# Adapter plus MoE MLP on one core: POOL, ScalarE and VectorE work reordered at one step of the first pair, adapter matmuls moved at one step of the second

## Chip, core and metric

One NeuronCore of a Trainium2 chip runs the whole kernel. The metric is the device time of one execution in microseconds. Five engines are named as the profile names them: PE (TensorE), DVE (VectorE), ACT (ScalarE), POOL (GpSimd) and SP (SyncE, which here only issues DMAs). Each runs its own queue of instructions strictly in order; they meet through semaphores alone.

## What is computed

16 sequences of 512 tokens by 512 features (f32) go through two residual layers. Both pick weights by an id of the sequence.

```
# layer 0, weights by language id
h = relu(x @ W1[lang] + b1[lang])                # 512 -> 128
y = x + h @ W2[lang] + b2[lang]
x = x + layernorm(y) * gamma[lang] + beta[lang]
# layer 1, last 128 output columns by expert id
h = gelu(x @ W1 + b1)                            # 512 -> 2048
x = x + concat(h @ W2 + b2, h @ We[expert] + be[expert])   # 384 + 128
```

## The kernel before

**Precision.** Every f32 operand of a matmul is split in two fp32r parts: `hi`, the value rounded (a cast, mostly on ACT), and `lo`, the value minus `hi` (a subtraction on DVE, some on POOL). A product is then three matmuls, hi x hi, hi x lo, lo x hi (lines 277 to 279). So before PE can use a tile, ACT must have cast it and DVE have subtracted it.

**Order of the work.** The 16 sequences are taken as 8 pairs, and each pair in 8 groups (k = 0 to 7) of the 2048 hidden features. The up projection of a group uses a Strassen-like scheme with seven products, P1 to P7, of six matmuls of 128 x 128 x 512 each: on PE, `pe_step` (line 576) issues P1, P5, then down products of an earlier group (`pe_down`, 24 matmuls for one sequence of the pair), P6, P2, P3, P7, down products again, P4. The seven products want sums of weight blocks (S1 to S4) and of input blocks (T1 to T4).

**First pair.** In it, the weights are prepared for all pairs: SP loads w1(k+1) raw (`load_w1_raw`, L1610 to L1613), POOL makes its four sums (`pool_weight_sums`, L1410 to L1415), ACT casts (`act_w1_hi`, L755), DVE subtracts (`dve_w1_lo`, L1082), SP stores the split weights in DRAM (`keep_w1`, L1620), from where later pairs load them. Two slots (k % 2) take turns, and a raw load waits for the store of the step before last and for P4 of k - 1. w2 goes the same way (`act_w2_hi` L759, `dve_w2_lo` L1087, `keep_w2` L1636); the expert's columns are split by POOL (`pool_expert`, L1397 and L1399).

**The next pair's layer 0.** While PE is at pair i, layer 0 of pair m = i + 1 is computed in between. At k = 0 to 3, four chunks of x transposed per sequence are loaded (`load_xT`, L1533; two slots, so chunk 2 waits until the products on chunk 0 and 1 are done), cast (L669), subtracted (`dve_xT_lo`, L912), and multiplied in pairs (`pe_adapter_ups`, 6 matmuls into the bank `aux`). The table `ADAPTER_UP` gives sequence and chunk for each n. At k = 2 to 5 follow the second adapter products and DVE's addition (`dve_add_adapter`, L925), which takes x + b2 from `x1`. POOL puts it there (`pool_biases`, L1330, L1332: two additions a tile, x + b2 and x + beta). DVE then takes the moments, finishes the layernorm a step later (`dve_finish`, L985), and turns the result in blocks of 32 x 32 (`dve_turns`, L1003). SP stores the turned tiles in DRAM (`keep_turned`, L1657, eight DMAs for a sequence) and later loads them as the transposed blocks B11 to B22 (L1677) of pair m.

**What sets the order around the change.** All orders are written out by hand: one function per engine and step. At the first pair, k = 5:

- POOL (`pool_first_step`, line 1424): both expert parts of k = 4, biases of tiles 2 and 3 of sequence 1, weight sums of w1(6), expert part of k = 5.
- ACT (`act_step`): gelu and cast of C11(5), cast of w1(6), C12, C22, cast of w2(5).
- DVE (`dve_first_step`): the sums C12 and C22, the low part of g C11(5), two finishes (L985), `dve_add_adapter` for tiles 2 and 3 of sequence 1, turns of tiles 2 and 3 of sequence 0, w1_lo(6), w2_lo(5), moments.
- SP: load of w1(6), store and loads of w2, `keep_turned` of sequence 0 (two halves, each waits for DVE's turns), then `keep_w1(5)`. At k = 6: load of w1(7), stores of w1(6) and w2(5), B11, turned tiles of sequence 1, w2(6), and at k = 7 the load of w1(8), by which pair 1 opens.

At pair 1, k = 1, PE runs P1, P5, the adapter up products on chunks 0 and 1 of pair 2, down(1,7) of the first pair, P6, P2, P3, P7. On DVE, at pair 1, k = 0, the order ends with:

```
        dve_g_lo(eng, i, k, C11)
        if m and k == 0:
            dve_xT_lo(eng, m, 0, 0)
            dve_xT_lo(eng, m, 0, 1)
        if k == 0:
            dve_g_lo(eng, before(i), GROUPS - 1, C12)
            dve_g_lo(eng, before(i), GROUPS - 1, C22)
```

and `pe_down` of sequence 1 waits for these two: `eng.wait_ge(dve_glo[b], pr.count(2 * GROUPS, 2 * k + h + 1))`.

Of the kernel before, what the change touches and what calls it, by code (L numbers as in the profile page):

```python
# [26 lines left out]
def build(nc, xT, x, lang, expert, a_w1, a_b1, a_w2, a_b2, a_gamma, a_beta,  # L27
# [153 lines left out]
    pairs = [Pair(n) for n in range(PAIRS)]  # L181
    first, last_pair = pairs[0], pairs[-1]
# [48 lines left out]
    def before(i):  # L231
        return pairs[i.index - 1]

    def seven(i, n):

        return max(0, i.count(GROUPS, n) - 1)
# [334 lines left out]
    def pe_adapter_ups(eng, m, n):  # L571
        b, c = ADAPTER_UP[n]
        pe_adapter_up(eng, m, b, c)
        pe_adapter_up(eng, m, b, c + 1)

    def pe_step(eng, i, m, k):
        if i is first and k == 0:
            pe_first_group(eng, i)
            return
        pe_p1(eng, i, m, k)  # L580
        pe_p5(eng, i, m, k)
        if m and i is not first and k == 1:
            pe_adapter_ups(eng, m, 0)
        if k % 2 == 0:
            if k >= 2:
                pe_down(eng, i, 0, k - 1)
            elif i is not first:
                pe_down(eng, before(i), 0, GROUPS - 1)
        else:
            if k >= 2:  # L590
                pe_down(eng, i, 1, k - 2)
            elif i is not first:
                pe_down(eng, before(i), 1, GROUPS - 1)
        pe_p6(eng, i, m, k)
        pe_p2(eng, i, k)
        if i is first and k == 1:
            pe_adapter_ups(eng, m, 0)
        pe_p3(eng, i, k)
        pe_p7(eng, i, k)
        if m and k in (2, 3):  # L600
            pe_adapter_ups(eng, m, k)
        if m and k in ADAPTER_DOWN:
            b, t = ADAPTER_DOWN[k]
            eng.wait_ge(act_gelu, i.count(4 * GROUPS, 4 * k + C11 + 1))
            pe_adapter_down(eng, m, b, t, up_a)
            eng.wait_ge(dve_c12, seven(i, k + 1))
            pe_adapter_down(eng, m, b, t + 1, up_c)
        if k % 2 == 0:
            if k >= 2:
                pe_down(eng, i, 1, k - 2)  # L610
            elif i is not first:
                pe_down(eng, before(i), 1, GROUPS - 2)
        elif i is last_pair and k == GROUPS - 1:

            pe_down(eng, i, 0, k - 1, (0,))
            pe_p4(eng, i, k)
            pe_down(eng, i, 0, k - 1, (1,))
            return
        else:
            pe_down(eng, i, 0, k - 1)  # L620
        if m and k == 1:
            pe_adapter_ups(eng, m, 1)
        pe_p4(eng, i, k)
# [133 lines left out]
    def act_w2_hi(eng, k):  # L757
        eng.wait_ge(in_w2[k % 2], 16 * (k // 2 + 1))
        eng.copy(w2[:, k % 2, :, HI, PART:D], w2_raw[:, k % 2, :, LO, PART:D]).then_inc(act_w2hi, 1)  # L759
# [35 lines left out]
    def act_step(eng, i, m, k):  # L795
        if i is first and k == 0:
            return
        if i is first and k == 1:
            act_second_step(eng, i, m)
            return  # L800
        if k > 0:
            act_g(eng, i, k - 1, C21)
        elif i is not first:
            act_g(eng, before(i), GROUPS - 1, C21)
        if i is not first and k < GROUPS - 1 and (k > 0 or before(i) is not first):
            load_w1(eng, i, k + 1)
        act_seed_b(eng, i, k)
        if k > 0:
            act_keep_p5(eng, i, k)
        if k == 1:  # L810
            act_keep_u2(eng, i, k)
        if i is first and k % 2 == 1:
            act_w2_hi(eng, k - 1)
        if k == 0 and before(i) is first:
            act_next_blocks(eng, i)
        if k == 0 and i is not first:
            if before(i) is not first:
                for c in range(2):
                    act_t_hi(eng, i, T3, c)
            for c in range(2):  # L820
                act_block_hi(eng, i, B22, c)
            if before(i) is first:
                load_w1(eng, i, k + 1)
                for c in range(2):
                    act_t_hi(eng, i, T3, c)
            act_keep_p5(eng, i, k)
            if m:
                act_aw_hi(eng, m, 0, 0)
            act_keep_u2(eng, i, k)
            for c in range(2):  # L830
                act_t_hi(eng, i, T4, c)
        if m:
            if k in (2, 4):
                act_relu(eng, m, k // 2 - 1)
            if k in (1, 2, 3):
                b, c = ADAPTER_UP[k]
                act_xT_hi(eng, m, b, c)
                act_xT_hi(eng, m, b, c + 1)
            if k > 0 and k in ADAPTER_WEIGHTS:
                act_aw_hi(eng, m, *ADAPTER_WEIGHTS[k])  # L840
            if k == GROUPS - 1:
                for c in range(2):
                    act_block_hi(eng, m, B11, c)
                if i is not first:
                    load_w1(eng, m, 0)
        if k > 1:
            act_keep_u2(eng, i, k)
        if i is first and k == GROUPS - 1:
            act_w1_hi(eng, k + 1)
        act_g(eng, i, k, C11)  # L850
        if i is first and k < GROUPS - 1:
            act_w1_hi(eng, k + 1)
        if m and k == GROUPS - 1:
            for c in range(2):
                act_t_hi(eng, m, T1, c)
        if m and k == 0:
            act_xT_hi(eng, m, 0, 0)
            act_xT_hi(eng, m, 0, 1)
        act_g(eng, i, k, C12)
        if i is first and k == GROUPS - 1:  # L860
            act_w2_hi(eng, k)
        act_g(eng, i, k, C22)
        if i is first and k in (3, 5):
            act_w2_hi(eng, k)
        if m and k == GROUPS - 1 and i is not first:
            act_next_blocks(eng, m)
# [138 lines left out]
    def dve_turns(eng, m, b, t):  # L1005
        dve_turn(eng, m, b, t)
        dve_turn(eng, m, b, t + 1)
# [77 lines left out]
    def dve_w2_lo(eng, k):  # L1085
        eng.wait_ge(act_w2hi, k + 1)
        eng.tensor_tensor(w2[:, k % 2, :, LO, PART:D], w2_raw[:, k % 2, :, LO, PART:D],  # L1087
                          raw(w2[:, k % 2, :, HI, PART:D]), ALU.subtract).then_inc(dve_w2, 1)
# [27 lines left out]
    def dve_first_step(eng, i, m, k):  # L1116
# [51 lines left out]
        if k in ADAPTER_DOWN:  # L1168
            b, t = ADAPTER_DOWN[k]
            dve_add_adapter(eng, m, b, t, up_a)  # L1170
            dve_add_adapter(eng, m, b, t + 1, up_c)
        if k == 5:
            dve_turns(eng, m, 0, 2)
        if k == 2:
            dve_g_lo(eng, i, k - 1, C22)
            dve_g_lo(eng, i, k, C11)
# [22 lines left out]
            dve_turns(eng, m, 0, 0)  # L1199
        if k == 5:  # L1200
            dve_w2_lo(eng, k)
            dve_moments(eng, m, b, t)
        if k == 6:
            dve_g_lo(eng, i, 5, C12)
# [219 lines left out]
    def pool_first_step(eng, i, m, k):  # L1424

        if k == 0:
            for c in range(2):
                pool_t_lo(eng, i, T1, c)
            return
        if k == 1:  # L1430
            pool_expert(eng, i, 0, 1)
            eng.wait_ge(aw_split, m.front(4, 1))
            pool_aw_lo(eng, m, 0, 1)
            pool_expert(eng, i, 1, 0)
            pool_weight_sums(eng, 3)
            return
        if k == 2:
            pool_biases(eng, m, 0, 0)
            pool_biases(eng, m, 0, 1)
            pool_expert(eng, i, 1, 1)  # L1440
            pool_biases(eng, m, 0, 2)
            pool_biases(eng, m, 0, 3)
            return
        pool_roots(eng, m, k)
        if k == 3:
            pool_expert(eng, i, 0, 2)
            pool_weight_sums(eng, 4)
            pool_expert(eng, i, 1, 2)
            pool_expert(eng, i, 0, 3)
            pool_first_bias(eng, 0)  # L1450
            return
        if k == 4:
            pool_biases(eng, m, 1, 0)
        if k % 2 == 1:
            pool_expert(eng, i, 0, k - 1)
            pool_expert(eng, i, 1, k - 1)
        else:
            pool_expert(eng, i, 1, k - 1)
        if k == 5:
            pool_biases(eng, m, 1, 2)  # L1460
            pool_biases(eng, m, 1, 3)
        if k == 4:
            eng.wait_ge(aw_split, m.front(4, 3))
            pool_aw_lo(eng, m, 1, 1)
        pool_weight_sums(eng, k + 1)
        if k == 4:
            pool_biases(eng, m, 1, 1)
            pool_first_bias(eng, 1)
        if k == GROUPS - 1:
            pool_first_w1_lo(eng, 2)  # L1470
            pool_first_w1_lo(eng, 3)
            pool_expert(eng, i, 0, k)
            pool_expert(eng, i, 1, k)
        elif k % 2 == 1:
            pool_expert(eng, i, 0, k)
# [599 lines left out]
```

## Time and profile before

| | |
|---|---|
| runs | 1422.74, 1424.14, 1424.50 us |
| median | 1424.14 us |
| the profiled execution | 1424.01 us |
| its span (first to last instruction) | 1422.2 us |
| PE busy | 1413.5 us (99%) |
| DVE busy | 878.6 us (62%) |
| ACT busy | 588.0 us (41%) |
| POOL busy | 619.2 us (44%) |
| granted TensorE clock, mean | 0.999 |
| HBM traffic | 205 GB/s over the span |

The times of all rows are microseconds from the first instruction of the span; L and a number is a line of the kernel. PE, DVE, ACT and POOL are the engines, SPq the issue of a DMA on SP. `g`, `w`, `xTs` and so on are the names of tiles. A matmul's duration (0.39) is longer than the distance from one start to the next (0.227), since matmuls are pipelined; it is the distance that counts.

### The profile page before, as it was taken

The page shows a single profiled execution, that of the slowest core. Times are in us where ns is not written, and L with a number is a line of the kernel's source. Part 1 is how long each engine was busy: PE and PEld are TensorE (multiplying, and loading weights), DVE is VectorE, ACT ScalarE, POOL GpSimd, SP SyncE. Part 2 cuts the span into 40 slices and gives each one's busy share as a digit, 9 for nine tenths or more (in the row PEclk, how much of TensorE's full clock was granted, in tenths as well). Part 3 has the DMA queues.
Part 4 walks back from the last instruction along what each step waited for, and adds up shares of the span by engine and source line. Part 5 has one row for each costly group of instructions (what it writes and reads, how often), then busy time and mean ns, then how long its engine had stood idle before and what let it go on. Part 6 is the DMA issues. An engine that isn't in the chain of part 4 may idle for free.

```text
span 1422.2 us, 18606 instructions
## 1 busy us (share of the span) xinstructions
PE 1413.5 (99%) x6220; PEld 1163.1 (82%) x6220; DVE 878.6 (62%) x1472; ACT 588.0 (41%) x968; POOL 619.2 (44%) x628
## 2 busy tenths in 40 slices
PE   9999999999999999999999999999999999999999
PEld 6888787888888888888888888888888888888887
DVE  6888785665656756567565675556665576543333
ACT  4843455333543335343343434443345333533231
POOL 5279345451473414734257342563334633351101
PEclk9999999999999999999999999999999999999999
DMA  8755997558765687566774677645876458654332
GB/s 272 254 183 181 236 357 261 173 170 210 255 218 187 173 233 251 196 211 174 232 254 154 211 193 246 239 151 196 228 245 244 150 173 222 201 191 163 134 111 89
DMA packets 273955, 292.37 MB, mean 206 GB/s; under 512 B 129602, under 2 KB 230722, under 8 KB 265796
## 3 DMA queue, kind: packets, MB, share of 16 engines
q1 hardware_dynamic: 264068, 188.15, 44.7%
q10 hardware_dynamic: 9792, 103.03, 19.2%
q8 instruction: 50, 0.82, 0.2%
q14 instruction: 45, 0.37, 0.1%
HBM read 238.70 MB, written 52.43 MB: 205 GB/s over the span
## 4 chain that ended last, share of the span: by engine, by line
PE 94%; SPq 2%; DVE 2%; DMA 2%; issue 0%; POOL 0%; ACT 0%; ACTq 0%; DVEq 0%
PE down L278 15%; PE down L277 15%; PE down L279 15%; PE up_b L278 5%; PE up_b L277 5%; PE up_b L279 5%; PE up_c L277 4%; PE up_c L278 4%; PE up_c L279 4%; PE up_a L278 4%; PE up_a L277 4%; PE up_a L279 4%; SPq L1657 1%; PE aux L277 1%; PE aux L279 1%; PE aux L278 1%
## 5 line engine op out<-in xcount | busy, mean ns | idle before, releaser
L883 DVE TENSOR_TENSOR g<-g_raw,g 128x512 fp32r<-128x512 f32 x256 | 227.5, 916 | 283.8 <-ACT g L664 283.8
L277 PE MATMUL down<-w,g 128*128 128x512 f32 x1024 | 399.0, 390 | 0.1
L278 PE MATMUL down<-w,g 128*128 128x512 f32 x1024 | 398.8, 389 | 0.0
L279 PE MATMUL down<-w,g 128*128 128x512 f32 x1024 | 398.7, 389 | 0.0
L1397 POOL CAST w<-w_raw 128x256 fp32r<-128x256 f32 x125 | 69.8, 559 | 533.0 <-DMA w_raw<-m_we 532.9
L277 PEld LDWEIGHTS down<-w,g 128*128 128x128 f32 x1024 | 192.8, 188 | 41.1 <-DVE w L1087 0.9
L279 PEld LDWEIGHTS down<-w,g 128*128 128x128 f32 x1024 | 192.3, 188 | 40.0
L278 PEld LDWEIGHTS down<-w,g 128*128 128x128 f32 x1024 | 192.5, 188 | 39.8
L638 ACT COPY u<-up_b 128x512 f32<-128x512 f32 x63 | 37.1, 589 | 304.9 <-PE up_b L279 285.2
L664 ACT CAST g<-g_raw 128x512 fp32r<-128x512 f32 x256 | 159.0, 621 | 8.1
L656 ACT ACTIVATE g_raw<-u,m_b_sb 128x512 f32<-128x512 f32 x63 | 45.6, 723 | 236.8 <-PE down L279 221.0
L277 PE MATMUL up_b<-bo,w 128*128 128x512 f32 x336 | 130.7, 389 | 0.0
L278 PE MATMUL up_b<-bo,w 128*128 128x512 f32 x336 | 130.7, 389 | 0.0
L279 PE MATMUL up_b<-bo,w 128*128 128x512 f32 x336 | 130.7, 389 | 0.0
L1399 POOL TENSOR_TENSOR w<-w_raw,w 128x256 fp32r<-128x256 f32 x128 | 113.4, 886 | 28.2 <-ACT w L765 18.2
L906 DVE TENSOR_TENSOR resid<-down,resid 128x512 f32<-128x512 f32 x124 | 81.0, 684 | 39.2 <-PE down L279 39.2
L656 ACT ACTIVATE g_raw<-up_b,m_b_sb 128x512 f32<-128x512 f32 x63 | 43.2, 686 | 137.0 <-PE up_b L279 137.0
L279 PE MATMUL up_c<-bo,w 128*128 128x512 f32 x224 | 87.2, 389 | 0.0
L278 PE MATMUL up_c<-bo,w 128*128 128x512 f32 x224 | 87.1, 389 | 0.0
L277 PE MATMUL up_c<-bo,w 128*128 128x512 f32 x224 | 87.1, 389 | 0.0
L1332 POOL TENSOR_TENSOR xs<-xs,vecs 128x512 f32<-128x512 f32 x56 | 81.6, 1457 | 4.4
L873 DVE TENSOR_TENSOR u<-up_c,u 128x512 f32<-128x512 f32 x63 | 43.5, 690 | 62.2 <-PE up_c L279 55.7
(234 smaller groups left out, 2414.7 us busy)
## 6 DMA issues: line engine op xcount, KB each, us to landing
w<-w_kept ACTq DMA_DIRECT2D x55, 1792.0 KB, 7.5
w<-w_kept SPq DMA_DIRECT2D x56, 768.0 KB, 5.1
w_raw<-m_we SPq DMA_DIRECT2D x128, 128.0 KB, 4.6
out<-resid SPq DMA_DIRECT2D x64, 256.0 KB, 4.7
xTs_raw<-xT SPq DMA_DIRECT2D x56, 256.0 KB, 3.0
xs<-x SPq DMA_DIRECT2D x56, 256.0 KB, 6.3
w_kept<-w SPq DMA_DIRECT2D x8, 1792.0 KB, 8.1
x_turned<-turned SPq DMA_DIRECT2D x112, 128.0 KB, 3.4
```

The costliest lines, as they stand in the source:

```text
L277: eng.matmul(bank, a_hi, b_hi, start=opens, stop=False, skip_group_check=True)
L278: eng.matmul(bank, a_hi, b_lo, start=False, stop=False, skip_group_check=True)
L279: return eng.matmul(bank, a_lo, b_hi, start=False, stop=closes, skip_group_check=True)
L638: eng.copy(u2[:, :], up_b[:, :]).then_inc(act_u2, 1)
L656: eng.activation(values, source, ACT.Gelu, bias=m_b1_sb[:, j:j + 1]).then_inc(act_gelu, 1)
L664: eng.copy(g[:, b, k % 2, h, HI, :], values).then_inc(act_ghi[b], 1)
L873: eng.tensor_tensor(u2[:, :], up_c[:, :], u2[:, :], ALU.add).then_inc(dve_c12, 1)
L883: eng.tensor_tensor(g[:, b, k % 2, h, LO, :], g_raw[:, b, k % 2, h, LO, :], raw(g[:, b, k % 2, h, HI, :]), ALU.subtract).then_inc(dve_glo[ ...
L906: eng.tensor_tensor(resid[:, 1, t, :], down[t][:, :], before_sum[:, 1, t, :], ALU.add).then_inc(dve_out[1], 1)
L1332: eng.tensor_tensor(xs[:, t, :], xs[:, t, :], vec_tile(m, b, BETA), ALU.add).then_inc(pool_xb, 1)
L1397: eng.tensor_copy(hi, values).then_inc(pool_eh[b], 1)
L1399: eng.tensor_tensor(lo, values, raw(hi), ALU.subtract).then_inc(pool_e[b], 1)
```

## The change

Five edits. At the first pair's k = 5: (1) POOL makes the weight sums of w1(6) between the biases of tile 2 and those of tile 3; (2) ACT casts w2(5) right after C11, ahead of w1(6); (3) DVE turns tiles 2 and 3 of sequence 0 after the low parts of w1(6) and w2(5), where it turned them before both. At pair 1's k = 1: (4) PE issues the adapter up products behind P2 instead of behind P5, so after down(1,7) and P6. (5) A constant, `LATE = 2`, names the pairs with the later place; the first pair had it already.

```diff
+    LATE = 2
+
     def pe_step(eng, i, m, k):
...
         pe_p1(eng, i, m, k)
         pe_p5(eng, i, m, k)
-        if m and i is not first and k == 1:
+        if m and i not in pairs[:LATE] and k == 1:
             pe_adapter_ups(eng, m, 0)
...
         pe_p6(eng, i, m, k)
         pe_p2(eng, i, k)
-        if i is first and k == 1:
+        if m and i in pairs[:LATE] and k == 1:
             pe_adapter_ups(eng, m, 0)
         pe_p3(eng, i, k)
         pe_p7(eng, i, k)
...
         act_g(eng, i, k, C11)
+        if i is first and k == 5:
+            act_w2_hi(eng, k)
         if i is first and k < GROUPS - 1:
             act_w1_hi(eng, k + 1)
...
         act_g(eng, i, k, C22)
-        if i is first and k in (3, 5):
+        if i is first and k == 3:
             act_w2_hi(eng, k)
...
             dve_add_adapter(eng, m, b, t, up_a)
             dve_add_adapter(eng, m, b, t + 1, up_c)
-        if k == 5:
-            dve_turns(eng, m, 0, 2)
...
         if k == 5:
             dve_w2_lo(eng, k)
+            dve_turns(eng, m, 0, 2)
             dve_moments(eng, m, b, t)
...
         if k == 5:
             pool_biases(eng, m, 1, 2)
-            pool_biases(eng, m, 1, 3)
         if k == 4:
             eng.wait_ge(aw_split, m.front(4, 3))
             pool_aw_lo(eng, m, 1, 1)
         pool_weight_sums(eng, k + 1)
+        if k == 5:
+            pool_biases(eng, m, 1, 3)
```

## Rows read from the trace of the kernel before

**Rows 1.** The page: busy time of PE, and the chain that ended last, by engine.
```profile
PE 1413.5 (99%) x6220; PEld 1163.1 (82%) x6220; DVE 878.6 (62%) x1472; ACT 588.0 (41%) x968; POOL 619.2 (44%) x628
PE 94%; SPq 2%; DVE 2%; DMA 2%; issue 0%; POOL 0%; ACT 0%; ACTq 0%; DVEq 0%
```

**Rows 2.** Waits of PE: who waited for whom, us in total, times, longest.
```profile
PE aux L277 <- DVE xTs L912: 2.4, 1, 2.4
...
PE up_a L319 <- DVE w L1082: 0.8, 1, 0.8
```

**Rows 3.** PE's timeline, first pair, k = 5 to 6: start, us, instruction, idle before.
```profile
147.40 0.39 PE L279 MATMUL up_b<-bo,w 128*128 128x512 f32 x1
...
149.77 0.74 PE L319 MATMUL up_a<-bo,w 128*128 128x512 f32 x2 [0.81 <-DVE w L1082]
...
151.98 0.50 PE L277 MATMUL down<-w,g 128*128 128x512 f32 x1
```

**Rows 4.** PE's timeline, pair 1, k = 1.
```profile
213.36 0.39 PE L279 MATMUL up_c<-bo,w 128*128 128x512 f32 x1
216.19 0.47 PE L277 MATMUL aux<-xTs,aw 128*128 128x512 f32 x1 [2.44 <-DVE xTs L912]
...
227.42 0.39 PE L277 MATMUL up_c<-bo,w 128*128 128x512 f32 x1
```

**Rows 5.** Stretches: length, then busy us of PE, PEld, DVE, ACT, POOL, then granted clock.
```profile
213.40:221.10 7.70, 5.25 (x17) 3.91 (x16) 3.84 (x6) 5.93 (x10) 0.72 (x2) 0.78 0.98 357
```

**Rows 6.** The chain of waits in order of time, 139 to 216: start, us, what.
```profile
146.24 0.30 SPq L1657
...
148.52 6.43 DMA w_kept<-w
...
176.68 0.56 SPq L1610
...
191.59 1.42 DVE w L1087
...
205.51 9.17 DMA xTs_raw<-xT
```

**Rows 7.** POOL's timeline, first pair, k = 5.
```profile
139.11 1.30 POOL L1330 TENSOR_TENSOR x<-xs,vecs 128x512 f32<-128x512 f32 x1
...
142.07 1.19 POOL L1410 TENSOR_TENSOR w_raw<-a,w_raw 128x256 f32<-128x256 f32 x1
...
145.18 0.74 POOL L1415 TENSOR_TENSOR w_raw<-w_raw 128x256 f32<-128x256 f32 x1
...
146.34 0.74 POOL L1399 TENSOR_TENSOR w<-w_raw,w 128x256 fp32r<-128x256 f32 x1
```

**Rows 8.** ACT's timeline, the cast of w1(6).
```profile
145.96 1.70 ACT L755 CAST w<-w_raw 128x1792 fp32r<-128x1792 f32 x1 [7.67 <-POOL w_raw L1415]
```

**Rows 9.** DVE's timeline, first pair, k = 5.
```profile
144.33 0.68 DVE L925 TENSOR_TENSOR x<-up_c,x 128x512 f32<-128x512 f32 x1
144.93 1.29 DVE L1003 STREAM_TRANSPOSE turned<-x 128x512 f32<-128x512 f32 x2
147.69 2.03 DVE L1082 TENSOR_TENSOR w<-w_raw,w 128x1792 fp32r<-128x1792 f32 x1 [1.47 <-ACT w L755]
150.97 0.96 DVE L1087 TENSOR_TENSOR w<-w_raw,w 128x768 fp32r<-128x768 f32 x1 [1.26 <-ACT w L759]
```

**Rows 10.** PE's timeline, the first down product at pair 1, k = 0.
```profile
193.06 0.50 PE L277 MATMUL down<-w,g 128*128 128x512 f32 x1
```

**Rows 11.** Line L1082 over the run: duration in ns, least, median, most.
```profile
L1082 DVE TENSOR_TENSOR w<-w_raw,w x7: 1984/2015/3107, 38.9 to 166.9; 128x1792 fp32r<-128x1792 f32 x7
```

**Rows 12.** DVE's timeline, pair 1, k = 0, behind the xT splits.
```profile
216.64 1.28 DVE L883 TENSOR_TENSOR g<-g_raw,g 128x512 fp32r<-128x512 f32 x2
```

**Rows 13.** First pair, k = 1: SP's loads of xT, ACT's casts of them.
```profile
47.17 0.81 SPq L1533 DMA_DIRECT2D xTs_raw<-xT  x2
...
51.92 1.14 ACT L669 CAST xTs<-xTs_raw 128x512 fp32r<-128x512 f32 x2
```

## The prediction

> **What bounds the kernel now.** I read the page first. TensorE (PE) is busy for 1413.5 of 1422.2 us and holds 94% of the chain that ended last [rows 1]. So the end moves only where PE gains or loses time. The next view is the list of what PE waited for. It is short: the longest wait is 2.4 us for a low part of xT (DVE L912), and 0.8 us stands for a low part of w1 (L1082) [rows 2]. The change touches both, and everything after them is PE at its own pace, so a microsecond won or lost here reaches the end whole. Something over 0.2% (2.85 us) is what a measurement of this kernel can tell from no change.
>
> PE's pace is 0.227 us a matmul. In the first pair, up to down(1,5) of k=6, PE starts a matmul at 147.40; thirteen paces on would be 150.35, but the thirteenth starts at 151.98 [rows 3]. So **stall A** costs 1.63 us: P1 waited for the low part of w1(6), the down products for that of w2(5). At pair 1, k=1, the last matmul of P5 starts at 213.36 and the 43rd after it (first of P3) at 227.42 where 43 paces give 223.11 [rows 4]. So **stall B** costs 4.31 us. Only 2.6 of these are the wait; about 1.7 are matmuls at the half clock: the granted clock of 213.4 to 221.1 is 0.78, half of it at 1.2 GHz after the idle time, where it is full elsewhere [rows 5].
>
> The third view is the chain of waits in order of time. It leaves PE at k=5 of the first pair and comes back only at stall B. The links are: the two turns of batch 0 end at 146.2; SP issues their stores (L1657), then the store of w1(5), which lands after 6.43 us; only then may SP load w1(7); SP issues without rest until w1(8) at 176.68; then POOL's sums, ACT's and DVE's splits, among them w2_lo(7) at 191.59; then at 205.51 the load of xT(0,0), 9.17 us [rows 6]. I take from this that the turns of batch 0, tiles 2 and 3, start a path of 60 us in which nearly nothing waits for anything outside it.
>
> **The change, part by part.**
>
> *The weight sum before the last bias.* POOL's stretch is bias(1,2) from 139.11, bias(1,3) to 142.1, four sums from 142.07 to 145.92, then the expert's parts [rows 7]. Swapped, the sums take 3.85 us and end at about 143.0, and bias(1,3) ends where the sums ended, at 145.9; POOL's total doesn't change. ACT's cast of w1(6), 1.7 us [rows 8], is then done at 144.7 in place of 147.7. But DVE's add_adapter(1,3) waits for bias(1,3) (pool_xb, both of its additions), and it stands ahead of w1_lo in DVE's queue. It ran at 144.33 [rows 9]; now it runs at 145.95 to 146.6. So the gain of 3 us on ACT reaches DVE as one of about 1.1: w1_lo(6) takes 2.03 us and ends at 148.6 instead of 149.7.
>
> *w2_hi(5) earlier on ACT, w2_lo(5) behind w1_lo(6).* ACT is idle there, so the 0.8 us cost nothing; w2_lo(5) takes 0.96 [rows 9] and ends at 149.5. P1 of k=6 wants its low part four paces after 147.62, at 148.5, and the down products want w2_lo at 150.35. So stall A shrinks from 1.63 to 0.1: **gain 1.5 us**, at that place.
>
> *The turns behind the low parts.* They took 1.29 us from 144.93 [rows 9]. Now they come last: 145.95 + 0.68 (add) + 2.03 + 0.96 + 1.29, less 3 x 0.08 by which such instructions overlap, is 150.65, against 146.22. SP gets them **D = 4.4 us later**. What is queued behind that wait on SP is what the chain shows: the four stores, the store of w1(5), and behind its landing the loads of w1(7), w2(6) and w1(8). Each takes its time again, so w2_lo(7) ends at 193.01 + 4.4 = 197.4. The down products of the first pair's k=7 began at 193.06, directly after it, with no slack [rows 10]. PE thus stands 4.4 late there whatever stall A gave back: the 1.5 us are swallowed. The bounds of D: 2.9 if add(1,3) waited for nothing (then only 2.0 and 0.96 stand before the turns); 5.5 if w1_lo took the 3.11 us it once took beside POOL [rows 11]. I take 4.4 because the median of the seven w1_lo is 2.02.
>
> Beside it stands a rule. Here w1_lo would start at 146.6, when POOL's split of the expert weights (146.34, 0.74 us [rows 7]) has begun. The Trainium skill, "SBUF — State Buffer", section "SBUF: two separate sides", says that a DVE instruction with two SBUF inputs and a GpSimd one that reads SBUF take one port pair as an exclusive lock: whoever starts first keeps it for the whole instruction. By it w1_lo would start at 147.1 and D be 4.9; the 3.11 us row agrees that DVE can be held up, and the range holds it.
>
> *Adapter up products behind P2 (pair 1, k=1).* PE's order becomes down(1,7), P6, P2, up products, P3. The 24 + 6 + 6 matmuls give xT 8.2 us more. But down(1,7) needs the low part of g C12(7), and in DVE's queue that split stands directly **behind** the two xT splits: it starts at 216.64, the first of two [rows 12], and is done at 217.3. So in the old frame PE, free at 213.6, now waits until 217.35 instead of 216.19. The wait isn't removed, it is 1.16 us longer. From the restart to P3 the work is 42 matmuls either way, 9.52 us; with the same 1.7 us of half clock P3 begins at 217.35 + 9.52 + 1.71 = 228.58 against 227.42: **cost 1.16**. DVE's own path to 216.64 goes through w2_lo(7) and the load of xT, so it carries D too.
>
> Behind that, the load of xT(0,2) waits for the moved products (they free its slot), and the next up products come only P3 + P7 + down(0,0) = 36 matmuls = 8.16 us later, not 16.3. In the first pair, where the order is already so, SP issued this load at 47.17 and ACT split it at 51.92 [rows 13]; 4.75 + 1.14 + 1.28 is under 8.16, so I cost it at nothing. With the 9.17 us of rows 6 in its place it would be 11.4, a stall of some 3 us.
>
> **Sum.** Stall A -1.5, but +1.5 again before 193 (the low part of w2(7) decides); D +4.4; the new wait +1.2: +5.6 us. The profiled execution took 1424.01 us, 0.1 under the median of the runs (1424.14) and 1.8 longer than its span. 1424.0 + 5.6 = **1429.6 us**.
>
> **The rivals.**
> 1. *Forecast, 0.62*: 1429.6. Its own range is D's 2.9 to 5.5, and 2 us more or 1.7 less for the clock: 1426.4 to 1432.7.
> 2. *SP's path has slack for D* (the stores of turned tiles and of w1(5) go faster when nothing else moves, or w1(7) isn't what the later steps wait for). Then only the longer wait at down(1,7) is left: 1424.0 + 1.2 = 1425.2. For it: the 6.43 us of the store of w1(5) were shared with the turned tiles, so one link can shrink; against it: the chain has no wait outside SP and its transfers from 146 to 177. 0.13.
> 3. *xT lands sooner*: with 4.75 us in place of 9.17 the splits come 4.4 earlier, the g split is ready when PE comes 4.4 late, and stall B is gone: 1424.0 + 4.4 - 4.3 = 1424.1, no change. Against it: the same queue of loads stands before it, moved as a whole. 0.07.
> 4. **Faster.** The mechanism is the one of parts 1 and 4 together: w1(8) and w2(7) aren't late, and xT's splits are no longer what PE meets, as DVE's order would allow if they had been done before 213.6. Then stall B goes whole: 1424.0 - 4.3 = 1419.7. It decides if w2_lo(7) is less than 1.4 us late (so that less than that is given back of 4.3) and the g split is done by then. Against it: rows 10 and 12. 0.10.
> 5. *The second xT load is late as well* (9.17 us landing): 1429.6 + 2.8 = 1432.4. 0.08.
>
> Faster is case 4, same (1421.3 to 1427.0) cases 2 and 3, slower cases 1 and 5. The range reaches down to case 3, and up a little past case 5: 1423.8 to 1433.5; it leaves out case 4 and the tails of 1 and 5.
>
> **What would show it.** In the changed profile: L1082 of k=6 at about 146.6; the third and fourth turns at 149.4; SP's store of w1(5) near 153 and the load of w1(8) near 181; PE waiting for several low parts of the first pair between 168 and 198 (w1(7), pool's w1 split, w2(7)); the list of PE's waits headed by down at pair 1 for g (L883), near 3.7 us, none for xTs. Wrong if the load of w1(8) is issued before 178, or if PE finds the g split done at pair 1, k=1. If PE loses more than D on the way to 198, that excess isn't added but taken out of the wait for g.

## The result and the profile after

| | before | changed |
|---|---|---|
| runs | 1422.74 to 1424.96 us (5) | 1429.94 to 1431.56 us (5) |
| median | 1424.16 us | 1431.51 us |
| profiled execution | 1424.01 us | 1430.64 us |
| its span | 1422.2 us | 1428.8 us |

The ratio is 1.0049, with a 95% interval of 1.0034 to 1.0063: the changed kernel is slower by about 7 us (7.0 by the ratio, 7.4 by the medians). The forecast was 1429.6, the range 1423.8 to 1433.5.

The page of the changed kernel, the two lines that answer to [rows 1]:

```profile
PE 1414.8 (99%) x6220; PEld 1162.6 (81%) x6220; DVE 877.2 (61%) x1472; ACT 587.9 (41%) x968; POOL 622.7 (44%) x628
PE 92%; DVE 3%; SPq 2%; DMA 1%; POOL 1%; issue 1%; ACT 0%; DVEq 0%; POOLq 0%
```

PE's work is the same, its share of the chain is two points smaller. Where it went stands in the list of PE's waits (who waited for whom, us in total, times, longest), which answers to [rows 2]:

```profile
PE down L277 <- DVE g L887: 4.2, 1, 4.2
...
PE down L277 <- DVE resid L910: 1.6, 1, 1.6
PE up_a L319 <- DVE w L1086: 1.3, 2, 0.8
PE down L277 <- DVE w L1091: 0.9, 1, 0.9
PE up_a L314 <- ACT w L757: 0.5, 1, 0.5
PE up_c L332 <- POOL w L1358: 0.2, 1, 0.2
```

The wait for xT is gone, and a longer one stands in its place: down products that wait for the low part of g. (Lines of the changed kernel are 2 to 4 further down: L887 is before's L883, L1086 its L1082, L1091 its L1087, L1661 its L1657, L1614 its L1610.) Six smaller ones lie between 149 and 198.

Now the path that starts with the turned tiles. POOL at k = 5 of the first pair, for [rows 7]:

```profile
139.75 0.73 POOL L1413 TENSOR_TENSOR w_raw<-a,w_raw 128x256 f32<-128x256 f32 x1
...
142.41 1.07 POOL L1418 TENSOR_TENSOR w_raw<-w_raw 128x256 f32<-128x256 f32 x1
143.45 1.75 POOL L1333 TENSOR_TENSOR x<-xs,vecs 128x512 f32<-128x512 f32 x1
145.28 1.30 POOL L1335 TENSOR_TENSOR xs<-xs,vecs 128x512 f32<-128x512 f32 x1
...
147.00 0.73 POOL L1402 TENSOR_TENSOR w<-w_raw,w 128x256 fp32r<-128x256 f32 x1
```

DVE in the same stretch, for [rows 9]:

```profile
146.68 0.69 DVE L929 TENSOR_TENSOR x<-up_c,x 128x512 f32<-128x512 f32 x1 [2.04 <-POOL xs L1335]
147.29 2.33 DVE L1086 TENSOR_TENSOR w<-w_raw,w 128x1792 fp32r<-128x1792 f32 x1
149.54 0.94 DVE L1091 TENSOR_TENSOR w<-w_raw,w 128x768 fp32r<-128x768 f32 x1
150.41 1.29 DVE L1007 STREAM_TRANSPOSE turned<-x 128x512 f32<-128x512 f32 x2
```

The weight sums do end early, at 143.5, but DVE's second addition stands 2.04 us idle until POOL's last bias is done. Then come both low parts, then the turns, which end at 151.7; in the kernel before they ended at 146.2. SP's timeline, for the SP links of [rows 6]: the store of w1(5), the load of w1(8), and the load of xT(0,0).

```profile
154.01 0.62 SPq L1624 DMA_DIRECT2D w_kept<-w  x1
...
181.56 0.57 SPq L1614 DMA_DIRECT2D w_raw<-m_w  x1
...
210.41 1.41 SPq L1537 DMA_DIRECT2D xTs_raw<-xT  x2
```

Against 148.52, 176.68 and 205.51 these are 5.5, 4.9 and 4.9 us later. PE's timeline shows the end of the path, for [rows 4, 10]:

```profile
197.95 0.50 PE L277 MATMUL down<-w,g 128*128 128x512 f32 x1 [0.92 <-DVE w L1091]
...
218.29 0.39 PE L279 MATMUL up_c<-bo,w 128*128 128x512 f32 x1
222.85 0.47 PE L277 MATMUL down<-w,g 128*128 128x512 f32 x1 [4.17 <-DVE g L887]
...
234.05 0.39 PE L277 MATMUL up_c<-bo,w 128*128 128x512 f32 x1
```

And DVE's, with the order that causes it (for [rows 12]): the two xT splits, before which it stood idle for 7.26 us, and the two g splits behind them.

```profile
220.81 1.29 DVE L916 TENSOR_TENSOR xTs<-xTs_raw,xTs 128x512 fp32r<-128x512 f32 x2 [7.26 <-ACT xTs L671]
222.02 1.29 DVE L887 TENSOR_TENSOR g<-g_raw,g 128x512 fp32r<-128x512 f32 x2
```

The first g split is done at 222.7 and PE starts at 222.85: 6.66 us later than it restarted before (216.19). P3 starts at 234.05, against 227.42 [rows 4]: 6.63 later, which is also the difference of the two profiled executions. The half clock is there too; 222 to 230 has a granted clock of 0.79 (columns: length, busy us of PE, PEld, DVE, ACT, POOL, clock):

```profile
222.00:230.00 8.00, 7.15 (x25) 5.78 (x26) 5.81 (x9) 4.07 (x7) 4.21 (x5) 0.79 0.82 285
```

### The profile page after: what moved, and what is told of

The parts are those of the page before. It is cut to its first block, busy times and chain, and to the rows that moved or that the text cites. A ratio compares the mean times of both kernels' runs of the same rounds, so it can differ in the third digit from the quotient of the medians.

```text
span 1428.8 us, 18606 instructions
## 1 busy us (share of the span) xinstructions
PE 1414.8 (99%) x6220; PEld 1162.6 (81%) x6220; DVE 877.2 (61%) x1472; ACT 587.9 (41%) x968; POOL 622.7 (44%) x628
## 4 chain that ended last, share of the span: by engine, by line
PE 92%; DVE 3%; SPq 2%; DMA 1%; POOL 1%; issue 1%; ACT 0%; DVEq 0%; POOLq 0%
PE down L279 15%; PE down L277 15%; PE down L278 15%; PE up_b L279 5%; PE up_b L277 5%; PE up_b L278 5%; PE up_c L279 4%; PE up_c L277 4%; PE up_c L278 4%; PE up_a L279 4%; PE up_a L277 4%; PE up_a L278 4%; PE aux L277 1%; PE aux L279 1%; PE aux L278 1%; SPq L1661 1%
## 5 line engine op out<-in xcount | busy, mean ns | idle before, releaser
L887 DVE TENSOR_TENSOR g<-g_raw,g 128x512 fp32r<-128x512 f32 x256 | 227.2, 915 | 280.5 <-ACT g L666 280.5
L910 DVE TENSOR_TENSOR resid<-down,resid 128x512 f32<-128x512 f32 x124 | 81.0, 685 | 39.1 <-PE down L279 39.1
L1333 POOL TENSOR_TENSOR x<-xs,vecs 128x512 f32<-128x512 f32 x56 | 80.6, 1440 | 4.5 <-DVE resid L905 4.5
```

The lines of the kernel that those rows point to most:

```text
L887: eng.tensor_tensor(g[:, b, k % 2, h, LO, :], g_raw[:, b, k % 2, h, LO, :], raw(g[:, b, k % 2, h, HI, :]), ALU.subtract).then_inc(dve_glo[ ...
L910: eng.tensor_tensor(resid[:, 1, t, :], down[t][:, :], before_sum[:, 1, t, :], ALU.add).then_inc(dve_out[1], 1)
L1333: eng.tensor_tensor(x1[:, b, t, :], xs[:, t, :], vec_tile(m, b, B2), ALU.add).then_inc(pool_xb, 1)
```

## The experiments

Two profiled executions also differ in how late their opening is: SP's store of w2(4), which lies before any edit, is issued at 135.95 in the kernel before and at 136.60 in the changed one. In the table, events are therefore taken from that store and given as differences to the kernel before. The last two columns are the time: the ratio to the kernel before, run on the same chip in the same rounds, with its interval.

| run | turns end | w1(8) issued | xT issued | ratio | interval |
|---|---|---|---|---|---|
| changed | +4.8 | +4.2 | +4.3 | 1.0049 | 1.0034 to 1.0063 |
| e1 move of the products alone | 0.0 | -0.2 | -0.2 | 1.0009 | 1.0000 to 1.0018 |
| e2 changed, without the move | +4.8 | +5.0 | +5.8 | 1.0035 | 1.0023 to 1.0047 |
| e3 turns ahead of the low parts | +1.7 | +1.8 | +1.8 | 1.0036 | 1.0022 to 1.0050 |
| e4 g splits first, DVE alone | +4.8 | +4.9 | +6.0 | 1.0020 | 1.0011 to 1.0029 |
| e5 turns between the additions | -1.0 | -1.2 | -1.2 | 1.0010 | 1.0002 to 1.0019 |
| e6 turns ahead of the finishes | -3.9 | -1.4 | -1.4 | 1.0009 | 1.0000 to 1.0018 |
| e7 POOL's old order | +5.6 | +5.3 | +5.3 | 1.0057 | 1.0044 to 1.0070 |
| e8 changed, xT splits deferred | +4.8 | +4.6 | +4.6 | 1.0021 | 1.0012 to 1.0029 |
| e9 late turns alone | +6.9 | +6.5 | +6.5 | 1.0048 | 1.0034 to 1.0062 |
| e10 e6 without the move | -3.9 | -1.2 | -1.2 | 0.9994 | 0.9985 to 1.0003 |
| e11 move, xT splits deferred | 0.0 | +0.1 | +0.2 | 0.9977 | 0.9968 to 0.9987 |
| e12 e6, xT splits deferred | -3.9 | -1.4 | -1.3 | 0.9976 | 0.9965 to 0.9986 |

The changed kernel, e2, e4 and e8 run the same instructions up to the load of xT, and their four profiled executions issue it 4.3 to 6.0 late. So an entry of the third and fourth column is sure to a microsecond or so, no better. 0.001 of the ratio is 1.4 us; runs of different rounds are compared by their ratios.

**e1: the move alone.** From the kernel before:

```diff
-        if m and i is not first and k == 1:
+        if m and i not in pairs[:2] and k == 1:
             pe_adapter_ups(eng, m, 0)
...
-        if i is first and k == 1:
+        if m and i in pairs[:2] and k == 1:
             pe_adapter_ups(eng, m, 0)
```

> The kernel before with the move of the adapter up products behind P2 at pair 1, k = 1 alone. Theory (two terms: turned tiles handed to SP late, carried on to pair 1; and the moved products leave PE in front of the g split that stands behind the xT splits on DVE): only the second term is there, before + 1.2 us, about 1425.4; PE's longest wait is down on g, 3.8 us at about 213.6 to 217.4. Rival 1 (the move does what it is for, and the whole loss is the first pair's): before - 4.3, about 1419.9, no such wait. Rival 2 (the move makes the loss of the changed kernel, by a later second load of xT or a longer half clock): about 1430.

Measured: 1426.08 us, 1.4 over the kernel before in the same rounds (1424.72). PE's waits of this run:

```profile
PE down L277 <- DVE g L885: 3.8, 1, 3.8
```

Wait and price are those of the theory (the interval reaches from 0 to 2.6 us, so the price is known roughly). By itself the move makes nothing better: PE leaves one wait out and meets the next in DVE's queue. Rivals 1 (1419.9) and 2 (1430) are out.

**e2: the changed kernel without the move.** `LATE = 1` in the changed kernel.

> The changed kernel with the adapter up products of pair 1 back behind P5; the edits at the first pair, k = 5, stay. Theory: the late path alone, 1431.5 - 1.2 = 1430.3; PE waits about 2.5 us for the xT split at pair 1, k = 1, with the xT load issued near 210.4. Rival 1 (the loss is the first pair's, the move a gain of 4.3): about 1435. Rival 2 (the moved products make the loss): about 1424.

Measured: 1429.26 us, ratio 1.0035, 5 us over before. PE's longest wait but one is for xT again, as in [rows 2]:

```profile
PE down L277 <- DVE resid L910: 2.3, 1, 2.3
PE aux L277 <- DVE xTs L916: 2.0, 1, 2.0
```

The first pair's part is some 5 us, the move some 2 on top (0.0014 of 1424). The trace has the wait for xT back. The price of the move can't be taken from these two runs alone, since their intervals overlap.

**e3: the turns back in front.** From the changed kernel:

```diff
             dve_add_adapter(eng, m, b, t + 1, up_c)
+        if k == 5:
+            dve_turns(eng, m, 0, 2)
...
             dve_w2_lo(eng, k)
-            dve_turns(eng, m, 0, 2)
```

> The changed kernel with the turns of tiles 2 and 3 ahead of both low parts again, behind the second addition. Theory (the end follows the end of these turns, microsecond for microsecond): the turns end near 148.6 instead of 151.6, so 1431.5 - 3.0 = 1428.5, though the low part of w1(6) comes 1.2 later and PE loses that at k = 6. Rival (PE's stalls for low parts in the first pair are what costs, the path through SP is not): 1431.5 + 1.2 = 1432.7.

Measured: 1428.59 us; the intervals of this run and of the changed kernel overlap, so the step of 3 us isn't proved by the times alone (the ratios, 1.0036 and 1.0049, say 1.9). The trace has it: the turns end 3.1 earlier and the load of xT is issued 2.4 earlier (at 207.38), both against the store of w2(4). And the rival wanted a slower run, since w1_lo(6) came later (PE waited 1.34 us for it instead of 0.46). PE lost more at k = 6 and the kernel did not get slower.

**e7: POOL's old order.** In the changed kernel, both biases ahead of the weight sums again:

```diff
             pool_biases(eng, m, 1, 2)
+            pool_biases(eng, m, 1, 3)
...
         pool_weight_sums(eng, k + 1)
-        if k == 5:
-            pool_biases(eng, m, 1, 3)
```

> The changed kernel with POOL's old order (both biases, then the weight sums). Theory: the second addition comes 2 us earlier, but ACT's cast of w1(6) 3 us later, w1_lo ends at 149.7, w2_lo at 150.6, the turns at 151.9: the same as changed within 0.5 us, 1431.5 to 1432. Rival (the POOL swap is what makes the turns late): 1429 or less.

Measured: 1431.02 us, ratio 1.0057. So POOL's swap isn't what makes the turns late: without it ACT is what DVE waits for, and they come 0.7 later still.

**e9: the late turns alone.** The kernel before, `dve_turns(eng, m, 0, 2)` moved behind `dve_w2_lo(eng, 5)`, nothing else:

> The kernel before with one part alone: DVE's turns of tiles 2 and 3 behind w1_lo(6) and w2_lo(5) of k = 5. Theory (the end follows the turns): without the early casts w2_lo ends at 151.9, the turns at 153.1 in place of 146.2, so the load of w1(8) is issued near 183.5 and the time is before + 6.9. PE's wait for the xT split at pair 1 stays about 2.5 us. Rival (SP's path can give back some of it): less than before + 5, and a load of w1(8) before 181.

Measured: 1430.58 us beside 1423.19 for the kernel before, 7.4 over (6.8 by the ratio); the SP link:

```profile
183.30 0.56 SPq L1609 DMA_DIRECT2D w_raw<-m_w  x1
```

One moved instruction of DVE (two turns of 0.65 us) makes a loss as large as that of the whole changed kernel, 6.9 us late in and about 7 out, and the load of w1(8) was forecast to 0.2 us.

**e5: the turns in DVE's idle 2 us.** In the changed kernel:

```diff
             dve_add_adapter(eng, m, b, t, up_a)
+            if k == 5:
+                dve_turns(eng, m, 0, 2)
             dve_add_adapter(eng, m, b, t + 1, up_c)
...
             dve_w2_lo(eng, k)
-            dve_turns(eng, m, 0, 2)
```

> The changed kernel with the turns of tiles 2 and 3 between DVE's two additions, where it stands idle for 2 us (waiting for POOL's last bias). Theory (the end follows the end of the turns): they end at 145.9, as before, so nothing of the late path is left, and only the longer wait behind P5 at pair 1: before + 1.2, about 1425.5. Rival (POOL's new order, with the late second addition, costs in itself): 1429 or more.

Measured: 1424.50 us beside 1422.69: 1.8 over before, ratio 1.0010. Of the 7 us over before 1.4 are left by the ratio, what the move costs by e1. The turns ended not as in the kernel before but 1.0 earlier, and no gain from that shows. POOL's and ACT's new order are kept here; what they cost, if anything, lies within the interval of 1.3 us to either side.

**e6 and e10: the turns still earlier.** In the changed kernel, the turns ahead of `dve_finishes` of k = 5; e10 has `LATE = 1` besides.

> The changed kernel with the turns of tiles 2 and 3 ahead of DVE's finishes of k = 5; these tiles were finished a step before. Theory: the turns end near 142.9, SP is free for them at about 144 in place of 146.2, so the whole path starts 2.2 us earlier than in the kernel before: before - 2.2 + 1.2, about 1423.2. If something else than the turns holds SP's path (rival), no better than the turns between the additions, 1425.5.

> The turns ahead of the finishes, with the adapter up products of pair 1 behind P5 as in the kernel before; the other edits of the changed kernel stay. Theory: SP's path starts 1 to 1.5 us earlier than in the kernel before, and without the longer wait behind P5 that is all gain: before - 1.2. Rival (what PE meets at pair 1 isn't SP's path): before, within 0.3.

Measured: e6 1424.64 (ratio 1.0009), a miss: it was to be 1 us under the kernel before, and came out where the rival had it, level with e5. e10 1422.58 beside 1423.19 (ratio 0.9994); the interval reaches from 2.1 under to 0.4 over, so it holds both the expected -1.2 and the rival's 0. SP's timeline of e6 says why the path doesn't follow the turns any further:

```profile
139.72 7.84 SPq L1662 DMA_DIRECT2D x_turned<-turned  x8
147.60 0.75 SPq L1625 DMA_DIRECT2D w_kept<-w  x1
154.80 0.36 SPq L1615 DMA_DIRECT2D w_raw<-m_w  x1
```

The turns end at 143.1, but the eight stores take 7.84 us to issue without a break, and the store of w1(5) behind them lands 7.13 us after its issue, not 6.43. So w1(8) is 1.4 early, not 3.9. With the turns this early they aren't the limit, the issue of the stores is. This makes up 0.8 us of the miss (1.4 gained instead of 2.2). In the profiled execution the clock makes up some 1.7 more: over 21.6 us behind the start of the wait it was 0.84, where the kernel before has 0.92 (the last section has such rows).

**e4: DVE's order mended.** In the changed kernel, at pair 1, k = 0:

```diff
         dve_g_lo(eng, i, k, C11)
+        if k == 0 and before(i) is first:
+            dve_g_lo(eng, before(i), GROUPS - 1, C12)
+            dve_g_lo(eng, before(i), GROUPS - 1, C22)
         if m and k == 0:
             dve_xT_lo(eng, m, 0, 0)
             dve_xT_lo(eng, m, 0, 1)
-        if k == 0:
+        if k == 0 and before(i) is not first:
```

> The changed kernel with one more edit: at pair 1, k = 0, DVE splits g C12 and C22 of the first pair's k = 7 ahead of the xT splits. Theory (PE finds only this split missing): the wait of 4.2 us and 1.7 us of half clock behind it go, 1431.5 - 6.0 = 1425.5; the products on xT come 8 us later and find their split done. Rival (the xT load itself is what PE meets, or the next load of xT comes too late behind the moved products): the wait moves to the aux products, and the time falls by less than 3 us, 1428.5 or more.

Measured: 1426.91 us, ratio 1.0020. The wait for g is gone, and 4 us with it, more than the rival allowed and less than expected. The profiled execution was the slowest of the eleven (1432.29 us; the others end at 1427.75), so its trace shows what can happen and not what the median has. It has a third wait that neither named. PE's wait, and ACT's timeline:

```profile
PE up_b L277 <- ACT up_b L632: 3.1, 1, 3.1
```

```profile
223.11 1.29 ACT L671 CAST xTs<-xTs_raw 128x512 fp32r<-128x512 f32 x2 [9.35 <-DMA xTs_raw<-xT]
...
228.09 0.58 ACT L632 COPY up_b<-up_a 128x512 f32<-128x512 f32 x1
```

ACT's queue has the same fault as DVE's: six gelus and casts and the copy that opens P6 stand behind the casts of xT, which wait for the transfer. That load took 11.2 us in this execution, 9.7 in that of the changed kernel.

**e8: the xT splits deferred on both.** In the changed kernel:

```diff
-        if m and k == 0:
+        if m and k == 0 and i is not pairs[1]:
             act_xT_hi(eng, m, 0, 0)
...
+        if k == 1 and i is pairs[1]:
+            act_xT_hi(eng, m, 0, 0)
+            act_xT_hi(eng, m, 0, 1)
         if k == 1:
             act_keep_u2(eng, i, k)
...
-        if m and k == 0:
+        if m and k == 0 and i is not pairs[1]:
             dve_xT_lo(eng, m, 0, 0)
...
             dve_g_lo(eng, i, k - 1, C22)
+        if k == 1 and i is pairs[1]:
+            dve_xT_lo(eng, m, 0, 0)
+            dve_xT_lo(eng, m, 0, 1)
```

> The changed kernel with both splits of xT(0,0) and (0,1) out of the way at pair 1: ACT casts them at k = 1 behind the copy of P5, DVE subtracts them at k = 1 behind the splits of g C12 and C22. The run with DVE's order alone mended left a wait of 3.1 us at P6, for ACT's copy into up_b, which stood behind the casts of xT. Theory (what the move is for works once no queue has the splits in front): no wait between P5 and P3, after - 6.0, 1425.5. Rival (the xT load or the second load of xT is what PE meets): a wait at the aux products or at P4 of 2 us or more, 1427.5 or more.

Measured: 1426.39 beside 1422.69, ratio 1.0021: 4 us less than the changed kernel, not 6, and no less than e4 (1.0020). So the casts on ACT cost nothing that these times show (the intervals are 1.2 us to either side); they are shown to hold PE up only in the one long execution that e4's trace has. No wait is left between P5 and P3, one of 0.65 us stands at the down products behind them, and the late path is there (its six waits, at 152 to 201, are those of the changed kernel). By the sum, 4.6 of the path less 4.3 of stall B, e8 should be level with the kernel before or 1 us over; it is 3.0 over by the ratio (1.7 to 4.1), and what the rest is stays open.

**e11 and e12: versions that beat both.** e11 is e1 with the deferral of e8; e12 is e6 with it.

> The kernel before with the move of the products behind P2 and both splits of xT(0,0), (0,1) behind g C12 and C22 on ACT and DVE at pair 1; nothing changed at k = 5. Theory: no wait and no half clock at pair 1, k = 1: before - 4.3 at most, less up to 1 us for a wait behind the second load of xT. Rival (the wait only moves to a later product): before - 1 or more.

> All parts mended: POOL's and ACT's order of the changed kernel, the turns ahead of the finishes, the products behind P2, and the splits of xT out of the way on ACT and DVE. Theory: the 4.3 us of the wait at pair 1, and 1.1 to 1.5 us at k = 6 that SP's earlier path now lets PE keep: before - 5.5. If SP's path takes the second back, before - 4.3, as in the run without the edits at k = 5.

Measured, beside 1423.19: e11 1420.64 (0.9977), e12 1419.55 (0.9976, runs 1419.48 to 1420.60). Both beat the kernel before and the changed one, e11 by what was expected (4.3 less a new wait of about 1), e12 by less: its -5.5 lies outside its interval (-5.0 to -2.0), only the -4.3 of the other case lies inside. All that PE waits for in e12, with two waits of 1.7 and 0.7 in the opening:

```profile
PE up_a L319 <- DVE w L1089: 0.4, 1, 0.4
PE down L277 <- issue: 0.4, 1, 0.4
```

The last is the place where a new wait begins; in e11 it is 1.1 us long. PE starts there at 227.06, and POOL's timeline of e11 has, as the last thing before it, the split of the expert weights that down(0,0) waits for, itself late by its transfer:

```profile
225.64 0.40 POOL L1405 CAST w<-w_raw 128x256 fp32r<-128x256 f32 x1 [15.87 <-DMA w_raw<-m_we]
226.12 0.72 POOL L1407 TENSOR_TENSOR w<-w_raw,w 128x256 fp32r<-128x256 f32 x1
```

That this split is the cause is read from the order of times; no run moved it. Between e11 and e12 lie 1.1 us by the medians, but their intervals are nearly the same, so what the edits at k = 5 are worth once the turns are early stays within the noise.

## Why the prediction was right

The sign and both mechanisms held, the size roughly: the forecast of +5.6 came out as about +7.

- **The place of the turns.** Forecast: add(1,3) released by POOL's last bias, then w1_lo, w2_lo, the turns, D = 4.4. Measured from the common store: 4.8. Of the missing 0.4, 0.3 are in w1_lo, which took 2.33 us and not 2.03, and the rest in add(1,3), which began 0.1 later. (The row at 139.11 that the prediction calls bias(1,2) is the first of bias(1,3). It gave POOL's stretch the right length, so the sum isn't touched.) w1_lo was issued at 147.29 while POOL's split of the expert weights (147.00, 0.73 us) ran, and it ended 1.89 us after that split. The w1_lo of 3.11 us in the kernel before [rows 11] had begun beside a POOL addition too and ended 1.88 us after it:

```profile
74.96 3.11 DVE L1082 TENSOR_TENSOR w<-w_raw,w 128x1792 fp32r<-128x1792 f32 x1
```

```profile
74.45 1.74 POOL L1330 TENSOR_TENSOR x<-xs,vecs 128x512 f32<-128x512 f32 x1
```

  In e5 and e6, too, w1_lo began inside POOL's split and took 2.33; in e7 it began after it and took 2.03. This agrees with the rule of the Trainium skill, "SBUF — State Buffer", section "SBUF: two separate sides", that whichever of the two starts first keeps the ports for its whole instruction. By that rule the prediction had 4.9, the sum went by the row without it.
- **D carried through SP.** Right: +4.2 at w1(8), +4.3 at the load of xT, nearly all of 4.8. e9 is the clearest (6.9 in, 6.5 at xT, about 7 in the time), and the loads of e3, e5 and e7 move in step with their turns. The prediction's second rival (slack in SP's path) is out for delays. An earlier start is passed on only in part, by e6: 3.9 at the turns, 1.7 at the store of w1(5), 1.4 at w1(8).
- **Stall A.** Forecast 0.1 left. PE waited 0.46 at P1, and from the last matmul of P4 (147.91) to the first down product (151.62) it took 0.76 over its thirteen paces, so 0.9 of 1.6 us was won here, not 1.5. It was right that nothing of that gain would be kept: PE was at its down products at 197.95 behind w2_lo(7), as forecast, 4.9 late (4.2 from the common store).
- **Waits on the way.** Several between 168 and 198 were forecast: w1(7), POOL's split of w1, w2(7), and all three are there. The largest, 1.62 us at 186.6, was not among them: it is for DVE's down sums (L910), which stand in DVE's queue behind the late w2_lo(6) and free the bank. It changes nothing in the sum.
- **The move of the products.** Right in kind: the wait passes from xTs to g, and gets longer. Forecast 1.16; e1 gives 1.3, the pairs with and without it 2.0 and 2.1 (changed and e2, e6 and e10). Each of the three has an interval of a microsecond or more to either side, so 1.2 is not refuted. But a cause for more is in sight: the four traces with the wait for xT have a clock of 0.92 behind it, four of the six with the longer wait for g 0.84 (last section). The prediction took the same 1.7 us of half clock for both.
- **Rival 4, the faster one.** ACT's queue, with the same order as DVE's, was missed. It decides nothing in the changed kernel, since g's wait ends later. What the rival wanted, xT's splits out of PE's way, came with e11 and e12, by the ratios 3.3 and 3.4 us under the kernel before.
- **The second load of xT** (fifth rival): no run has a wait at its products. (Its price of 2.8 doesn't follow from the 11.4 and 8.16 that it is worked out from, which give 3.2.)
- **The rest**: the load of xT(0,0) took 9.73 us instead of 9.17, and the opening was 0.65 later. With these the profiled executions close: 0.65 (opening) + 4.25 (path to the load) + 0.56 (load) + 1.2 (the longer wait) = 6.66, the shift of PE's restart from 216.19 to 222.85.

The two terms of the sum thus came out as 4.25 and 1.2, where 4.4 and 1.2 were forecast. What made the profiled execution a microsecond longer than that was in no term: the opening and the longer load. How much of such terms an execution has is chance (the opening of e8's is 3.2 us late), so a fit closer than a microsecond would have been luck. The median of the changed kernel lies 0.9 over its profiled execution; no trace shows why, and the longer half clock of other runs is a candidate only.

## What to carry to other kernels

Before an instruction is moved back in its queue to make room for one that an idle engine seems to need, follow what it releases. Two turns of 0.65 us looked free to move, since no engine was named as waiting for them; but a DMA queue that works in order stood behind them, and it hands a delay on with all that is queued in it for 60 us (4.8 us in, 4.3 out). If a wait has to be hidden by putting work ahead of it, look up what that work waits for: here it waited for the same engine, behind the same late transfer. With the transfer's consumers put behind that work, the move gave its gain: e11 is 3.3 us under the kernel before, e1 1.3 over. Whether DVE's queue alone would have done is not shown on the kernel before; on the changed kernel DVE alone (e4, 1.0020) brought as much as both queues (e8, 1.0021).

## What the runs showed of the hardware

The half clock behind a wait doesn't come every time, and not always for as long. In e5's profiled execution PE stood idle for 3.29 us at pair 1, longer than the 2.44 us of the kernel before, and the clock stayed full:

```profile
212.00:226.00 14.00, 10.71 (x48) 8.56 (x46) 7.58 (x11) 6.53 (x11) 6.79 (x8) 1.00 0.83 303
```

That execution took 1422.36 us, the median of the kernel was 1424.50. In the kernel before and in e1, counted over 21.6 us:

```profile
213.40:235.00 21.60, 19.16 (x78) 15.43 (x77) 13.16 (x16) 11.88 (x20) 12.24 (x12) 0.92 0.85 306
```

```profile
214.40:236.00 21.60, 17.84 (x68) 14.29 (x67) 9.09 (x14) 8.74 (x15) 8.46 (x9) 0.84 0.69 236
```

Over such a stretch the clock was 1.00 in e5 (PE idle for 3.29 us), 0.92 in the kernel before (2.44), e2 (2.01), e9 (2.46), e10 (2.38) and the changed kernel (4.17), and 0.84 in e7 (3.01), e1 (3.75), e6 (3.88) and e3 (4.07). What is missing to 1.00 is lost: 0.08 of 21.6 us is 1.7 us, 0.16 is 3.5. So a wait of this length has three prices, nothing, 1.7 and 3.5 us beside its own length, and the length alone doesn't say which. It is a reason why a kernel with such a wait scatters, and e11 and e12, which have none, lie within 1.5 us (1419.72 to 1421.15, 1419.48 to 1420.60), the kernel before in the same rounds within 4 (1421.33 to 1425.32, one stray execution of 6942.77 left out). It is not the only one: e8 has no such wait at pair 1 and spreads over 3.2 us.

The opening varies as well. In e8's profiled execution everything up to the first pair's k = 5 was 3.2 us later than in the kernel before, with the same instructions, and its clock of 7 to 45 us was 0.96 (1.00 in the kernel before):

```profile
7.00:45.00 38.00, 37.47 (x152) 24.11 (x150) 29.07 (x56) 21.19 (x37) 21.15 (x31) 0.96 0.81 255
```

The times of a profile can therefore be compared only from a common event behind the opening, as in the table.
